# VectorE reads the value sums out of PSUM itself, and ScalarE's copies of them are dropped

## What is computed

```python
x = x + 0.5 * ffn(layernorm(x))
x = x + attn(layernorm(x))
x = x + 0.5 * ffn(layernorm(x))

def attn(x):                       # Tlen = 1024, HEAD_DIM = 8, N_HEAD = 16
    latent = x @ Wc_down
    q = (latent @ Wq_up).reshape(Bsz, Tlen, N_HEAD, HEAD_DIM)
    kv = latent @ Wkv_up
    k, v = kv[..., :HEAD_DIM], kv[..., HEAD_DIM:]
    att = jnp.einsum('bthd,bsd->bhts', q, k) * scale
    att = jnp.where(causal, att, -jnp.inf)
    att = softmax(att)
    y = jnp.einsum('bhts,bsd->bthd', att, v).reshape(Bsz, Tlen, C)
    return y @ Wc_proj

def ffn(x):                        # a fixed 128 x 128 matrix, made from w_freq
    return real(ifft(fft(x) @ w_freq)) + bias
```

## Time and profile before

| | |
|---|---|
| runs | 616.23, 618.06, 618.11 us; median 618.06 |
| the profiled execution | 615.98 us, its span 613.9 us |
| TensorE busy | 583.8 us (95%) |
| VectorE busy | 490.0 us (80%) |
| ScalarE busy | 380.2 us (62%) |
| GpSimd busy | 89.4 us (15%) |

### The profile page before, as it was taken

One profiled execution on the slowest core, in us unless ns is written; L12 is line 12 of the kernel. 1 busy time (PEld: TensorE's weight loads), 2 busy tenths in 40 slices (PEclk: granted clock), 3 DMA queues, 4 the chain that ended last, 5 costly groups with the idle time before them and its releaser, 6 DMA issues.

```text
span 613.9 us, 13365 instructions
## 1 busy us (share of the span) xinstructions
PE 583.8 (95%) x5205; PEld 325.9 (53%) x5205; DVE 490.0 (80%) x1258; ACT 380.2 (62%) x834; POOL 89.4 (15%) x311
## 2 busy tenths in 40 slices
PE   7676999999999999999999999999999999999898
PEld 6553664655454555545454546454545555453257
DVE  3762899998889899888899899798888989886023
ACT  2323148366777576776668776857676767677751
POOL 4202111110011312310012312100002110000100
PEclk8878999999999999999999999999999999999899
DMA  6011110011000010011010110011000100000000
GB/s 181 5 42 61 80 47 5 3 44 44 21 24 20 14 55 18 4 34 67 26 40 1 46 40 3 18 32 76 11 31 17 43 3 18 3 4 2 0 18 19
DMA packets 16978, 18.68 MB, mean 30 GB/s; under 512 B 2428, under 2 KB 14556, under 8 KB 16916
## 3 DMA queue, kind: packets, MB, share of 16 engines
q1 hardware_dynamic: 16243, 17.47, 8.4%
q10 hardware_dynamic: 672, 0.36, 0.2%
HBM read 11.90 MB, written 5.24 MB: 28 GB/s over the span
## 4 chain that ended last, share of the span: by engine, by line
PE 82%; ACT 7%; DVE 5%; issue 3%; DMA 1%; POOL 1%; SPq 1%; ACTq 0%; DVEq 0%
PE o_ps L764 22%; PE s1p L714 20%; PE st L738 20%; PE st L742 4%; PE s1p L717 4%; ACT probs L858 4%; PE misc L644 4%; PE st L750 3%; ACT z L840 2%; PE misc L639 1%; DVE mx_pair L1027 1%; DMA wkv<-in_w_kv 1%; PE misc L674 1%; SPq L591 0%; DVE mx L1027 0%
## 5 line engine op out<-in xcount | busy, mean ns | idle before, releaser
L858 ACT ACTIVATE probs<-st 128x512 f32<-128x512 f32 (+2 forms) x640 | 307.3, 564 | 141.1 <-PE st L742 87.3
L1027 DVE TENSOR_REDUCE mx_pair<-s1p 128x1 f32<-128x512 f32 (+3 forms) x432 | 260.2, 660 | 44.1 <-PE s1p L714 33.7
L714 PE MATMUL s1p<-k_sb,q_sb 72*128 72x512 bf16 (+3 forms) x768 | 220.4, 331 | 7.2 <-issue 4.3
L738 PE MATMUL st<-q_sb,k_sb 75*128 75x512 bf16 (+3 forms) x768 | 217.0, 328 | 5.5 <-ACT probs L858 3.6
L764 PE MATMUL o_ps<-probs,v_sb 128*32 128x512 f32 (+3 forms) x1536 | 145.9, 498 | 0.0
L714 PEld LDWEIGHTS s1p<-k_sb,q_sb 72*128 72x128 bf16 x768 | 73.7, 100 | 84.2 <-DVE mx_pair L1027 26.8
L738 PEld LDWEIGHTS st<-q_sb,k_sb 75*128 75x128 bf16 x768 | 73.6, 97 | 81.4 <-ACT probs L858 37.9
L1027 DVE TENSOR_REDUCE mx<-s1p 128x2 f32<-128x256 f32 (+2 forms) x192 | 104.3, 593 | 14.7 <-PE s1p L717 14.0
L717 PE MATMUL s1p<-ident,causal 128*128 128x128 bf16 x512 | 100.8, 222 | 0.0
L742 PE MATMUL st<-causal,ident 128*128 128x128 bf16 x512 | 100.3, 220 | 0.0
L764 PEld LDWEIGHTS o_ps<-probs,v_sb 128*32 128x32 f32 x1536 | 40.4, 110 | 66.9 <-issue 58.4
(11 more groups left out here) (115 smaller groups left out, 342.1 us busy)
## 6 DMA issues: line engine op xcount, KB each, us to landing
q_sb<-q_parts_dram SPq DMA_DIRECT2D x31, 288.0 KB
q_parts_dram<-q_parts SPq DMA_DIRECT2D x24, 128.0 KB
x_sb<-in_x SPq DMA_DIRECT2D x8, 256.0 KB, 4.4
out<-out_sb SPq DMA_DIRECT2D x8, 256.0 KB, 2.3
q_sb<-mT SPq DMA_DIRECT2D x14, 24.0 KB
const<-in_consts SPq DMA_DIRECT2D x1, 320.0 KB, 5.0
q_sb<-q_parts SPq DMA_DIRECT2D x5, 32.0 KB
q_sb<-q_parts ACTq DMA_DIRECT2D x4, 32.0 KB
```

Of the source, the lines that this page charges most:

```text
L714: last = mm(ps[:, e * width:(e + 1) * width], queries[:, h0 + e, at:at + P], k_sb[0:ROWS, b, lo:lo + width], start=True, stop=not diagonal)
L738: last = mm(ps[:, e * w:(e + 1) * w], k_sb[0:ROWS_MAX, b, P * ki:P * ki + P], q_sb[0:ROWS_MAX, slot, c, h0 + e, first:BLK], start=True, st ...
L858: nc.scalar.activation(probs[:, s % PROBS, h0:h0 + per, 0:w], st[n % 3][:, 0:per * w].rearrange("p (e w) -> p e w", e=per), ACT.Exp, scale ...
L1027: v.tensor_reduce(dst, s1p[n % 3][:, 0:heads * width].rearrange("p (e w) -> p e w", e=heads), axis=AX.X, op=ALU.max).then_inc(s1_free, 1)
```

## The change

VectorE's transposition reads `o_ps` directly, waits for the chunk's last value sum (`pv_done`) and raises `o_taken` itself. ScalarE's copy, the two tiles `o_sb`, the item `take` and the semaphore `o_seen` are gone. In the planner `select` stands where `take` stood, and `taken_at` is now the reckoned end of the transposition on VectorE.

```diff
+LAST_GROUP = [max(s for s, g in enumerate(GROUP) if g[0] == n) for n in range(len(CHUNKS))]
...
         if ki == 4 * c + 3:
             def take():
-                self.items.append(("take", n))
-                done = self.on_act(self.pe, .6)
-                self.taken_at[n] = done + .1
-                self.at(done + .1, lambda: self.select(u, c))
+                self.select(n, u, c)
             self.at(self.pe + HAND, take)
 
-    def select(self, u, c):
+    def select(self, n, u, c):
         self.items.append(("do", "sel", (u, c)))
         self.sel_done.add((u, c))
-        self.selected(u, c, self.on_dve(self.pe, DVE_STEP["sel"]) + .1)
+        self.taken_at[n] = self.on_dve(self.pe, DVE_STEP["sel"]) + .1
+        self.selected(u, c, self.taken_at[n])
...
-        o_sb, mT = twice("o_sb", [P, 512]), twice("mT", [PARTS * GH * NT, P], bf16)
+        mT = twice("mT", [PARTS * GH * NT, P], bf16)
...
-                elif item[0] == "take":
-                    last = max(s for s, g in enumerate(GROUP) if g[0] == item[1])
-                    act.wait_ge(pv_done, last + 1)
-                    if item[1] >= 2:
-                        act.wait_ge(o_seen, item[1] - 1)
-                    copy(o_sb[item[1] % 2][:, :], o_ps[:, :]).then_inc(o_taken, 1)
...
             def attention_rows(u, c):
                 n, g = CHUNKS.index((u, c)), u % GROUPS
-                dve.wait_ge(o_taken, n + 1)
+                dve.wait_ge(pv_done, LAST_GROUP[n] + 1)
...
-                v.transpose(o_turned[c][:, g, :, :].rearrange("p n c -> p (n c)"), o_sb[n % 2][:, :]).then_inc(o_seen, 1)
+                v.transpose(o_turned[c][:, g, :, :].rearrange("p n c -> p (n c)"), o_ps[:, :]).then_inc(o_taken, 1)
...
-                dve.wait_ge(o_seen, CHUNKS.index((GROUPS * (j // 2) + GROUPS - 1, j % 2)) + 1)
+                dve.wait_ge(o_taken, CHUNKS.index((GROUPS * (j // 2) + GROUPS - 1, j % 2)) + 1)
```

More of the change, by code:

```diff
@@ L504, in macaron_program @@
         st_ready, exp_done = sem("st_ready"), sem("exp_done")
-        pv_done, o_taken, o_seen, yT_ready = sem("pv_done"), sem("o_taken"), sem("o_seen"), sem("yT_ready")
+        pv_done, o_taken, yT_ready = sem("pv_done"), sem("o_taken"), sem("yT_ready")
         m_ready, mT_ready, out_ready = sem("m_ready"), sem("mT_ready"), sem("out_ready")
```

## The result

The changed kernel takes 620.0 us (median of 20 runs, 618.79 to 624.09), the kernel before in the same session 616.65 (20 runs, 615.42 to 618.11). The ratio is 1.0065, with a 95% interval of 1.0052 to 1.0077: 3.35 us slower, where 1.7 us faster was forecast. The time lies inside the range, the sign is wrong. That it lies inside is luck: the forecast and its range started from 618.06, the median of three runs, and the kernel before has 616.65 over 20; moved along by these 1.41 us the range would end at 619.2.

The account below looks back on a forecast made before the run. It took TensorE to bound the middle, with short bursts of late exponentials. Gains of 0.61 + 0.46 + 0.33 + 0.3 = 1.7 us, all else at 0, took 618.06 to 616.4 us; range 612.6 to 620.6.

Parts of the forecast that it names:

- The last transposition: At the end of the kernel: without the last copy the transposition starts in its place, a gain of 0.61 us.
- The transposition's own time: On VectorE: left at 702 ns out of PSUM; 0.1 us dearer each would put 0.2 us on the path.
- The bank: Value sums' PSUM bank, now free only when the transposition ends: taken as 0, with 0 to 6.8 us as the ends.
- The reductions behind the transposition: On VectorE, those freeing the sweep-1 banks: each 0.70 us later for about two reductions' time, priced at 0.
- The four inner copies: Copies on the chain at 575.11, 558.77, 473.42 and 488.03: dropping them gains 0.46, 0.33, 0.3 and 0 us.
- What is moved: Part pricing when the bank is free, the reductions behind the transposition, and the rewritten order: each 0, with bounds.
- the new order: Whole order rewritten by the planner, shifting late exponentials: left at 0, about 3 us either way over three middle stretches.
- A: Rival: the bank is held too long and value sums wait for VectorE's queue; slower, 619.8 to 623.2 us, chance 0.2.
- My own test: Sign in the profile after: filler in the middle, where there was none, would show the bank held too long.
- The other test: Sign in the middle stretches: a change of more than 1.5 us each would make the new order the larger effect.

Follow-up runs that it names:

- before_take70_maxfirst: The kernel before, its planner reckoning the copy at 0.7 instead of 0.6 us, unit 6's maxima kept ahead of unit 8's query load: 616.8 us.
- the hold: Pair with the epilogue of batches 0 to 2 held in the planner until sweep 1 is 6 tiles into unit 4b+5: changed kernel 614.13 us, kernel before 616.8.
- the picked ones: Pair with the shortest of 2500 lists by the planner's own end for each kernel: changed kernel 612.38 us, kernel before, with its copies, 608.34.

## Why the prediction was wrong

The last transposition, right: 0.61 forecast, 0.61 measured, and two filler groups less.

The transposition's own time, right: 705 ns out of PSUM for 702 out of SBUF. The estimated 65 ns that would be added by the Trainium skill, "VectorE: DVE Perf Modes", section "The TRN2 errata — SBUF-src ops pay a fixed extra latency per instruction", did not appear: the mean of the 32 is 3 ns up, so here the measurement decides.

The bank, right, and by the reason given: 0 of 0 to 6.8. With the old place the runs had 7.3, in the copy's place one wait of 1.8 was left, that of the earlier trace rows, and the planner avoided this too.

The reductions behind the transposition, put at 0 since "TensorE has three such banks and VectorE isn't on the chain of the middle": wrong as a step. With a fixed list it is 5.0 us. It did no harm in the kernel after (0.2 us in that row of its waits), whose list was dealt anew.

The four inner copies, 1.1 us in all: not confirmed one by one, because the places at which they stood no longer exist in the new list.

The step that failed is the last of "What is moved": the new order, "which I have left at 0", with "about 3 us either way". It is the largest term: 5.6 us with the copies in it, part of which is what copies cost in a list not made for them; in the middle of the changed kernel 3.66 and 3.27 us. I sized it by the exponentials' 4.6% of the chain, that is by ScalarE's bursts. What it moves is not these. It moves epilogue and prologue steps, on VectorE, 90% busy, and on TensorE, to the front or to the back of the maxima that sweep 2 lives on; and behind late maxima stand the fillers, +2.87 us in each middle batch. That VectorE was not named on the chain of before said only that its list was well dealt, not that there was slack for all that might be put there: seven transpositions more cost 1.66 us a batch. The planner's own end, which needs no run, would have warned: 579.1 us before and 584.2 after, though it is no sure sign (`before_take70_maxfirst`).

Of the rivals, A was the one with the right sign, by a mechanism that did not occur. My own test would have misled me: "Filler in the middle, where there was none, would be A as well". The filler came, and no value sum waits for the bank. The other test was the right one: "wrong from the ground up if the middle stretches got shorter or longer by more than 1.5 us each: then the new order ... is the larger effect". They got longer by 3.66 and 3.27.

What stays open is the worth of the change without its list. Pairs with lists made alike give 2.7 us for it (the hold) and 4.0 against it (the picked ones), where the planner's own ends differ by 1.0 for it and 4.2 against. Above the planner's own end the changed kernel stands 1.7 and 0.1 us lower in these pairs, an estimate from the table whose scatter is larger than that; the end's 0.61 is all that was seen by itself. Open too is how the loss in the middle divides between VectorE's steps and TensorE's jobs.

## What to carry to other kernels

Where a program writes the order of the work from reckoned times, a change of one step's time deals all of it anew, and this can move more than the step does. So compare the two lists first: which long steps on the two fullest engines have changed sides of the result that the next phase waits for, and where filler has appeared; then run the edit with the old list and the new list without the edit. Try the new list's freedom on the old kernel too: here it was worth 8 us, and the edit was not needed for it.

## What the runs showed of the hardware that I had not expected

A 24 KB DMA that stands 2.8 us behind two loads of 288 KB on the same queue was waited for until 8.1 us after its issue; with it issued ahead of them TensorE's waits for all such transfers came to 0.3 us. One such wait of 4.80 us cost more than itself, since TensorE ran at 0.50 of its clock behind it (0.50 from 288 to 296, 0.76 from 296 to 304): three waits, 10.3 us in all, and 22 us of time.

VectorE's transposition of 128x512 f32 takes the same out of PSUM as out of SBUF, 705 and 702 ns.
